# A slot table for the feed-forward jobs replaced by a cost budget, and one elementwise product moved from VectorE to GpSimd

## The reference

```python
x = L0_attn_X
xn = _layernorm(x, axis=-1)
s = _L0_attn_ref(xn, Wq, Wk, Wv, Wo)      # softmax(rope(Q) rope(K)^T / 4, causal) V, then Wo
g = _silu(_L0_ffn_ref(xn, ...))           # x_up = x Wup^T, x_gate = x Wgate^T, silu(x_gate) * x_up, then Wdown
x = x + s * g
```

## Time and profile before

| | |
|---|---|
| median of 3 runs | 825.88 us (825.41 to 828.42) |
| the profiled execution | 825.88 us, span of its trace 824.1 us |
| TensorE matmuls busy | 785.3 us, 95% of the span |
| VectorE, ScalarE, GpSimd busy | 563.7, 497.7, 416.8 us (68, 60, 51%) |
| chain that ended last | TensorE 62%, VectorE 5%, GpSimd 2%, DMA 1% |
| DMA | 95.71 MB, 116 GB/s |

### The profile page before, as it was taken

How to read it: one execution, slowest core, us unless ns; L and a number is a source line. 1 busy time by engine, 2 the same in 40 slices (tenths; PEclk the granted TensorE clock), 3 DMA queues, 4 the chain that set the end, 5 groups by cost and what they waited for, 6 DMA issues and landing times.

```text
span 824.1 us, 14501 instructions
## 1 busy us (share of the span) xinstructions
PE 785.3 (95%) x5212; PEld 479.7 (58%) x5212; DVE 563.7 (68%) x1019; ACT 497.7 (60%) x684; POOL 416.8 (51%) x474
## 2 busy tenths in 40 slices
PE   3999999999998999999999999999999999999987
PEld 2678888888765555554555555555555555554435
DVE  3785555445367777777777777777777777776736
ACT  2455475363543667666676765777766677666562
POOL 4569848476580553411665434166453236745233
PEclk9999999999999999999999999999999999999999
DMA  9144442463541221333334453334344333445121
GB/s 322 52 154 128 154 157 78 142 183 131 192 93 52 54 76 53 103 92 118 84 86 118 132 170 99 92 106 128 105 119 139 98 103 98 123 127 182 50 95 58
DMA packets 61055, 95.71 MB, mean 116 GB/s; under 512 B 10360, under 2 KB 27448, under 8 KB 60984
## 3 DMA queue, kind: packets, MB, share of 16 engines
q1 hardware_dynamic: 59400, 92.94, 37.2%
q10 hardware_dynamic: 1584, 1.84, 0.7%
HBM read 57.54 MB, written 36.95 MB: 115 GB/s over the span
## 4 chain that ended last, share of the span: by engine, by line
PE 62%; DVE 5%; POOL 2%; ACT 1%; DMA 1%; issue 1%; SPq 0%; DVEq 0%; ACTq 0%; POOLq 0%
PE ps L1361 15%; PE ps L327 12%; PE ps L1339 11%; PE ps L1316 10%; PE ps L337 7%; PE ps L1402 3%; DVE ps L1615 2%; PE ps L1327 2%; DVE mx L1620 2%; POOL a_sb L382 1%; DMA scr_heads<-o_raw 1%; ACT y_sb L362 1%; DVE y_sb L374 1%; DMA q_s<-shift 0%; ACT a_sb L347 0%
## 5 line engine op out<-in xcount | busy, mean ns | idle before, releaser
L1504 ACT ACTIVATE probs<-ps 128x1024 f32<-128x1024 f32 (+1 forms) x320 | 291.5, 937 | 108.2 <-PE ps L1339 106.4
L1620 DVE TENSOR_REDUCE mx<-ps 128x4 f32<-128x512 f32 (+1 forms) x192 | 215.5, 1134 | 76.9 <-PE ps L1316 48.1
L1199 POOL TENSOR_SCALAR_AFFINE_SELECT probs<-probs 128x256 f32<-128x256 f32 (+1 forms) x192 | 92.8, 486 | 262.1 <-ACT probs L1504 261.0
L1615 DVE CUSTOM_DVE_ANT_0 ps<-ps,tri 128x384 f32<-128x384 f32 (+1 forms) x256 | 154.6, 647 | 30.8 <-PE ps L1316 30.4
L1361 PE MATMUL ps<-probs,v_ones 128*32 128x512 f32 (+3 forms) x1584 | 158.1, 489 | 0.3
L1339 PE MATMUL ps<-q_s,k_s 64*128 64x512 f32 (+3 forms) x768 | 143.5, 399 | 8.1 <-DVE mx L1615 2.3
L1316 PE MATMUL ps<-k_s,q_s 48*128 48x512 f32 (+3 forms) x768 | 137.2, 382 | 3.4 <-DVE mx L1620 1.6
L1339 PEld LDWEIGHTS ps<-q_s,k_s 64*128 64x128 f32 x768 | 68.2, 185 | 104.8 <-issue 69.0
L1316 PEld LDWEIGHTS ps<-k_s,q_s 48*128 48x128 f32 x768 | 69.3, 184 | 70.9 <-ACT probs L1504 50.0
L327 PE MATMUL ps<-xh,wug_hi 128*128 128x512 f32 x256 | 105.7, 413 | 3.7 <-DVE rot L850 1.9
L382 POOL TENSOR_TENSOR a_sb<-a_sb,u_sb 128x512 f32<-128x512 f32 x64 | 83.2, 1307 | 40.3 <-ACT u_sb L355 21.5
(11 more groups left out here) (145 smaller groups left out, 1050.7 us busy)
## 6 DMA issues: line engine op xcount, KB each, us to landing
scr_qk<-kinds SPq DMA_DIRECT2D x64, 256.0 KB, 2.5
q_s<-scr_qk SPq DMA_DIRECT2D x64, 128.0 KB, 2.8
k_s<-scr_qk SPq DMA_DIRECT2D x64, 128.0 KB, 3.0
scr_heads<-o_raw SPq DMA_DIRECT2D x30, 256.0 KB, 2.1
x_sb<-in_x SPq DMA_DIRECT2D x8, 512.0 KB, 5.5
scr_v<-v_st SPq DMA_DIRECT2D x16, 256.0 KB, 2.9
q_s<-scr_qk SPq DMA_DIRECT2D x64, 64.0 KB, 3.0
k_s<-scr_qk SPq DMA_DIRECT2D x64, 64.0 KB, 3.0
```

What stands on the lines that cost most here:

```text
L1199: pool.affine_select(out=part, in_=part, compare_op=ALU.is_ge, fill=0.0, base=0, pattern=pattern, channel_multiplier=-1).then_inc(cut, 1)
L1504: act.activation(probs[:, n % 2, p, :, 0:w], ps[:, bank:bank + 2, 0:w], ACT.Exp, scale=SCALE).then_inc(exp_ok, 1)
L1615: last = dve.tensor_tensor_reduce(part_of, part_of, sh.tri[:, CH - w:CH], 1.0, LOWEST, ALU.add, ALU.max, mx[:, v % 2, kind, h, i % TPC:i % ...
L1620: last = dve.tensor_reduce(out[:, :, pairs[0]:pairs[0] + n], ps[:, banks[0]:banks[0] + 2, 0:n * w].rearrange('p e (x k) -> p e x k', x=n), ...
```

## The change

1. The table of slots goes. In its place each job has a cost, and the loop spends a budget that grows evenly from round 5 to round `FFN_END` = 83. A round takes a job when the cost spent so far plus half the job's cost is within the budget, and takes no further one once it holds four (`MOST` + 1; five in the first five rounds). Pieces and rows count as cost spent.
2. In the first kind of chain 'piece' and 'sum' are one round earlier (offset 4, not 5), and 'out' too. This holds for chunks 0, 2 and 4.
3. `scale_heads(7)` goes from VectorE to GpSimd, in round 82, where the chain has its 'scale'. VectorE's copy of the function goes, and one wait in its `low_part` with it.

Nothing else is computed, and no instruction is added. Jobs of rounds 5 to 79 by kind, counting gate, up, quarter or piece as one and a turn as half:

| kind | before | now |
|---|---|---|
| 0 | 15 rounds with 1 | 8 with 1, 1 with 1.5, 6 with 2 |
| 1 | 12 with 1, 3 with 2 | 1 with 0 (round 31), 8 with 1, 6 with 2 |
| 2 | 15 with 1 | 11 with 1, 4 with 2 |
| 3 | 1 with 1 (round 18), 14 with 2 | 7 with 1, 8 with 2 |
| 4 | 15 with 2 | 1 with 0 (round 59), 7 with 1, 1 with 1.5, 6 with 2 |

The rounds of kind 4 with one are 9, 19, 39, 49, 64, 69 and 79. The last gate or up (`LAST_FEATURES`) is in round 75, before in 73. Of the last down turn, (7, 1), the four quarters stand before in rounds 77, 79, 79 and 80, now in rounds 80, 81, 81 and 82.

The diff:

```diff
--- before.py
+++ after.py
@@ -143,8 +143,8 @@
 FIN = ((LAST - 1, slice(0, CH)), (LAST, slice(0, CH // 2)), (LAST, slice(CH // 2, CH)))
 
 
-CHAIN = [{'load': -3, 'recip': -2, 'keep': -1, 'spread': 0, 'scale': 1, 'high': 2, 'low': 2, 'more': 3, 'piece': 5,
-          'sum': 5, 'out': 6},
+CHAIN = [{'load': -3, 'recip': -2, 'keep': -1, 'spread': 0, 'scale': 1, 'high': 2, 'low': 2, 'more': 3, 'piece': 4,
+          'sum': 4, 'out': 5},
          {'load': 5, 'recip': 6, 'keep': 7, 'spread': 8, 'scale': 9, 'high': 10, 'low': 10, 'more': 11, 'piece': 12,
           'sum': 12, 'out': 13}]
 chain_at = {}
@@ -167,9 +167,10 @@
     todo += [j for j in left_over if j[0] != 'down'] if n == NEARLY else gates_and_ups(n)
     turns = [('turn', n + 1, d) for d in range(DC)] if n + 1 < NCHUNK else []
     todo += turns + downs(n) if n > NEARLY else downs(n)[:QUARTERS] + turns + downs(n)[QUARTERS:]
-
-SLOTS, FIRST_SLOTS, LAST_SLOTS = ((1, 1, 1, 2, 2), (4,) * NR, (1, 2, 0, 0, 0))
-slots_at = lambda z: (FIRST_SLOTS if z < NR else LAST_SLOTS if z >= END else SLOTS)[z % NR]
+COST = {'turn': 0.45, 'gate': 1.4, 'up': 1.4, 'down': 1.4, 'piece': 1.4, 'rows': 0.2, 'divide': 1.0}
+EARLY_COST = 5.6
+FFN_END = NROUND - 2
+MOST = 3
 jobs_at = [[] for _ in range(NROUND)]
 for v in range(NU):
     jobs_at[NR * v + 2].append(('rows', v, 0))
@@ -180,14 +181,21 @@
 jobs_at[END + 2].append(('divide', LAST - 1, 0))
 for o in range(DC):
     jobs_at[END + 3 + o].append(('piece', LAST - 1, o))
+cost_of = lambda jobs: sum(COST[j[0]] for j in jobs)
+total = cost_of(todo) + sum(cost_of(jobs) for jobs in jobs_at[:END])
+done = 0.0
 for z in range(NROUND):
-    left = slots_at(z) - sum(j[0] == 'piece' for j in jobs_at[z])
+    budget = EARLY_COST * (z + 1) if z < NR else min(
+        total, EARLY_COST * NR + (total - EARLY_COST * NR) * (z + 1 - NR) / (FFN_END - NR))
+    done += cost_of(jobs_at[z]) if z < END else 0
     closed = False
-    while todo and left > 0 and not (closed and todo[0][0] == 'down'):
-        j = todo.pop(0)
+    while todo and done + COST[todo[0][0]] / 2 <= budget + 1e-9 and len(jobs_at[z]) < MOST + (z < NR) + 1:
+        j = todo[0]
+        if closed and j[0] == 'down':
+            break
         closed = closed or (j[0] == 'down' and ends_turn(j))
-        left -= 0.5 if j[0] == 'turn' else 1
-        jobs_at[z].append(j)
+        done += COST[j[0]]
+        jobs_at[z].append(todo.pop(0))
 assert not todo
 
 for z in range(NROUND - 1):
@@ -1268,7 +1276,7 @@
                     take_values(v)
                 if at(z, 'low') is not None and at(z, 'low') < LAST:
                     low_part(at(z, 'low'))
-                if at(z, 'scale') is not None and at(z, 'scale') < LAST:
+                if at(z, 'scale') is not None:
                     scale_heads(at(z, 'scale'))
                 if at(z, 'sum') is not None:
                     for o in range(DC):
@@ -1658,14 +1666,6 @@
                                          sh.half_down[:, o:o + 1], gate_of(LAST, o)[:, cols], ALU.mult,
                                          ALU.mult).then_inc(gated_ok, 1)
 
-            def scale_heads(ch):
-                dve.wait_ge(heads_in[ch % 2], 16 * DC * (ch // 2 + 1))
-                dve.wait_ge(spread_in[ch % 2], 16 * DC * (ch // 2 + 1))
-                for rows, o in parts_of(ch):
-                    last = dve.tensor_tensor(heads_of(ch)[rows, o], heads_of(ch)[rows, o], spread_of(ch)[rows, o],
-                                             op=ALU.mult)
-                last.then_inc(scaled, 1)
-
             def high_part(ch):
                 dve.wait_ge(scaled, ch + 1)
                 if ch == LAST - 1:
@@ -1675,7 +1675,6 @@
                 last.then_inc(high, 1)
 
             def low_part(ch):
-                dve.wait_ge(low, ch)
                 dve.wait_ge(high, ch + 1)
                 dve.wait_ge(scaled, ch + 1)
                 for rows, o in parts_of(ch):
@@ -1749,7 +1748,6 @@
                 if z == END + 3:
                     end_high(0)
                     end_low(0)
-                    scale_heads(LAST)
                     high_part(LAST)
                     low_part(LAST)
             take_heads(1)
```

## The result

The changed kernel takes 836.7 us (median of four runs, 835.7 to 840.2) against 825.6 us before (four runs on the same chip): a ratio of 1.015, with a 95% interval of 1.012 to 1.018. It is slower, as forecast. The profiled execution took 834.53 us and its span is 832.8 us, 8.7 us over the 824.1 us of before.

What follows compares the result with a forecast made beforehand. TensorE, busy 95% of the span, was taken as the bound, so only its waits could change. Terms -4.1 + 7.3 + 3.0 - 2.0 + 2.4 + 2.5 = +9.1 us on 825.88 gave 835.0 us, range 828 to 840.

Steps and rivals of the forecast that it cites:

- quarters out of the middle: Three quarters of the last down turn move behind the transpose of round 80, which is reached 4.1 us sooner.
- thin rounds: Rounds of kinds 3, 4 and 1 with fewer jobs wait for VectorE's read of the third tile: +7.3 us.
- late ends: Five more rounds end on a gate or fourth quarter, each delaying the next round by 0.6 us: +3.0 us.
- `load_rest`: Moves from round 75 to 77, removing round 76's row-load wait and lateness in two rounds behind it: -2.0 us.
- fuller rounds that gain: Rounds of kinds 0, 1 and 2 with two jobs cost what they saved elsewhere; no gain counted.
- cuts (T to `weigh`): From round 80's transpose (T), step 7's `weigh` starts 2.4 us later, its cuts queued behind `scale_heads(7)` on GpSimd.
- clock behind it: After TensorE's new wait ahead of step 7's `weigh`, a half-clock stretch costs 2.5 us, bounds 0 and 3.4.
- That the middle costs nothing: Rival: VectorE catches up in fuller rounds so thin ones don't wait; 824.7 us, chance 0.10.
- that the cuts don't bind: Rival: the spread reciprocals land 3 us earlier, so `weigh` is due at T + 20.5; 829.6 us, chance 0.08.
- That the clock stays up: Rival: no slow clock stretch, as rounds 81 and 82 are fuller; 832.5 us, chance 0.25.
- `load_more(5)` was not delayed: Answers a rival: `load_rest` delays `load_more(5)`, needed in round 78, by 1.5 us; 836.5 us, chance 0.09.
- The faster rival: Quarters fill the last rounds' idle time, clock never falls, cuts in time, middle free; 819.3 us, chance 0.03.

Runs made afterwards that it cites:

- kind 4 thin: Kernel before with slots by kind (2, 1, 1, 2, 1) in place of (1, 1, 1, 2, 2): median 831.2 us, ratio 1.0082.
- kind 3 thin: Kernel before with slots by kind (2, 1, 1, 1, 2), the job taken from kind 3: median 828.2 us, ratio 1.0032.
- the two runs with the product elsewhere: Changed kernel with `scale_heads(7)` back on VectorE, median 832.5 us; or on GpSimd one round later, behind the cuts of step 7, median 831.6 us.
- the run with rounds 63, 68 and 73: Kernel before with only three quarters moved to rounds 81 and 82, one taken from each of these rounds: median 821.6 us, ratio 0.9962.

## Why the prediction was right, point by point

The forecast of 835.0 us and the measured 836.7 (834.5 in the profiled run, to which the sum was made) lie close, in the middle of the range. The sum of +9.1 us met 8.7. (By the medians the change cost 11.1 us, 2.0 more than the sum.) That the total came so close is in part luck, since its terms missed both ways:

| term | forecast | measured (profiled runs) |
|---|---|---|
| quarters out of the middle | -4.1 | -4.1 |
| thin rounds | +7.3 | +7.0 |
| late ends | +3.0 | +1.5 |
| `load_rest` | -2.0 | -0.9 |
| pieces under an open down turn | not seen | +0.9 |
| turns of round 54 in 54 and 55 | not seen | +0.7 |
| half clock in round 60 | not seen | +0.7 |
| fuller rounds that gain | 0 | -0.7 |
| cuts (T to `weigh`) | +2.4 | +1.9 |
| clock behind it | +2.5 | +1.4 |

The measured terms are rounded and add up to 8.4, where the lengths from round 5 on give 8.5. Thin rounds, late ends, cuts and clock were put 3.4 us too high in sum; `load_rest` (1.1 us) and the rows not seen (2.3 us, less 0.7 for fuller rounds) were missing 2.7 us. That leaves 0.7. The range's upper edge doesn't come out of its own working: with the upper bounds of late ends and clock the sum gives 837.9, not 840.

*Thin rounds.* Seven rounds of kind 4 with one job at 0.42 us each (0.43 forecast), round 59 2.2 us (2.0), round 31 1.2 (1.4), kind 3 0.7 in sum (0.9). The reading of the earlier trace rows, that the jobs cover the read of the third tile and by how much, carried the forecast. The runs with kind 4 thin and with kind 3 thin show it in isolation.

*Late ends.* This is the step that was off. The measured price behind kinds 3 and 1 held (rounds 24, 34, 37, 42, 49 and 67: 0.5 to 0.6 us). But both kernels have six such ends, so the five more are all of kind 4, and there I had taken the same price without a row for it. It was 0.2 behind round 9, 0.3 behind 29, 0.1 behind 49, none behind 79 and 0.6 behind 69, 1.2 us in all where 3.0 were forecast. Two pieces follow behind 29, 49 and 69 alike, so they don't decide it; what does stays open. And the late end of round 76 was taken away twice, once in the count of six and once in the "two rounds behind it" of `load_rest`.

*`load_rest`.* The wait of the earlier trace rows went, as forecast. It is worth 0.9 us; the rest of the -2.0 was the double count and round 78, which I had put down to it. Round 78 is long for another reason, shown by moving the pieces: they share banks with a tile while a down turn keeps its own open. The changed kernel puts the pieces of round 38 into the same position, and that round grows from 7.48 to 8.27 us.

*From T on.* The chain held step by step: the spread sent at T + 14.45 (T + 15.1 before, 0.4 earlier forecast), the product begun at T + 19.4 (20.1 forecast), 2.49 us long, the cuts, `weigh` at T + 22.9 (23.4 forecast), TensorE's wait 2.58 (2.9). The 0.4 us that I had taken off for ScalarE's tanh are not shown: in the thirteen profiled runs the spread is sent anywhere between T + 14.1 and T + 16.0, and the changed kernel with the product on VectorE, alike up to there, has T + 16.0. That it is this queue, and nothing else in the end, the two runs with the product elsewhere show: round 84 is 3.9 and 3.6 us shorter and no other round changed. 2.6 of the 3.9 us are the wait and the remaining 1.3 the clock behind it, by difference. The forecast of the clock was too high by 1.1 us, within its bounds; and it left out the slow stretch behind round 59, which cost 0.7.

*The rivals.* That the middle costs nothing fell with the thin rounds, and that the cuts don't bind with the 2.58 us. That the clock stays up fell twice, in the end and behind round 59. `load_more(5)` was not delayed: round 78 has the same length in both kernels. The faster rival describes what the three quarters do alone: 819.3 us was its number, and the kernel with nothing but them has a median of 821.6. Part of that closeness is chance, since this kernel also pays 1.7 us of late ends that the rival left out.

So the change is made of parts that pull apart. By lengths from round 5 on, which leave the scatter of the start out: the quarters in the last rounds, with `load_rest`, are worth -4.3 us (-3.7 up to round 80 and -0.6 behind it, the run with rounds 63, 68 and 73); the changed kernel with the product back on VectorE stands at +4.6 (+5.2 and -0.6), so by difference the new distribution over the middle costs 8.8; and the product ahead of the cuts another 3.9. In sum +8.5, to rounding.

## What to carry to other kernels

A job between two others may be there as cover: before moving it, look how long after the read it covers the next tile is issued, for that margin is what a round may lose for free (1.05 us in round 39, of which a job of 1.36 was taken). On an in-order queue, place an operation by when its input lands; ahead of work that is ready, its wait for that input and its own duration are passed on to that work. And spreading work evenly is no aim in itself: fill the rounds that wait and leave the others as they are.

## What the runs showed of the hardware

The granted clock fell to half behind two short waits. In round 59 of the changed kernel, TensorE's two waits were 0.62 and 1.10 us, and it was busy for 2.87 us of four; behind them the clock was at half for 3.4 us. The run with that round emptied alone shows the same, with waits of 0.63 and 1.10 us and 2.27 us busy of four. Waits of much the same kind can also leave the clock as it was. In round 31, emptied too, TensorE waited 0.21, 0.88 and 0.26 us and was busy for 2.96 us of four, and the clock stayed at full:

```profile
444.00:448.00 4.00, 2.96 (x28) 1.44 (x24) 3.60 (x11) 2.88 (x4) 4.00 (x6) 1.00 0.40 121
```

The scatter between executions goes with the clock. The profiled run of the changed kernel had a mean granted clock of 0.995; sixteen others had 0.985 to 0.992 and took 835.2 to 841.1 us, the longer the lower the clock (0.992: 835.2 to 837.4, 0.985: 841.1). The kernel with the three quarters alone has no wait over half a microsecond in its last rounds, its clock lies between 0.995 and 1.0, and its eleven runs keep within 3.4 us.

Why one execution loses more of the clock than another was not shown, since the unprofiled runs have no trace. Two things scatter by microseconds in the profiled ones. One is the start of round 5, from 262.0 to 265.3 us. The other is the sending of the spread reciprocals, from T + 14.1 to T + 16.0. In the changed kernel a later spread would lengthen TensorE's wait ahead of the cuts, and its profiled run, at T + 14.45, is among the early ones. So the wait of 2.58 us may be at the low end of what this kernel usually pays, and the median lies 2.2 us above the profiled run; that the one explains the other is an inference.
